# Flamingo gated block on one core: ScalarE's squares before its bank copies, output tiles one unit later, x1's statistics over four steps, another tail and beginning

## The chip, the cores and the metric

The kernel runs on one core of one Trainium2 chip. The metric is the device time of one execution in microseconds. The times before are from three executions; the trace is that of a fourth, profiled one.

## The reference

For eight batches b and an input x of 512 channels by 2048 positions:

```python
x = x + tanh(g_xattn) * xattn(layernorm(x), ctx, mask)     # gives x1
x = x + tanh(g_ffn) * ffn(layernorm(x))                    # layernorms run along the 2048 positions

def xattn(qk, v, mask):       # in windows of 128 positions, 8 heads of 32
    q, k, val = Wq @ qk + bq, Wk @ qk + bk, Wv @ v + bv    # 256 x 512 weights
    attn = softmax(q^T k / sqrt(32), masked)
    return (Wo @ gelu(attn applied to val) + bo) * mask

def ffn(x):                   # each of the 512 rows is 4 streams of 512
    logits = rms_norm(x) @ [W_res, W_pre, W_post]^T + base # 16 + 4 + 4 numbers a row
    H_res = (1-g) * I + g * sinkhorn(H_res_logits / 0.1, 50 iterations)   # 4 x 4 a row
    H_pre, H_post = softmax(...), softmax(...)
    y = (sum_n H_pre[n] * x[n]) @ W_branch                 # 512 x 512
    return H_res @ x_streams + H_post (outer) y
```

The output of a row tile is thus, for each of its four streams i: sum over j of cmat[i,j] * x1[j] + ccon[i] + post[i] * y, with the residual and the gates folded into the coefficients.

## The kernel before

The work is cut into 32 chunks G (eight batches, four chunks of 512 positions; `NG`, `CH`) and each chunk into eight units (four windows, two halves of the heads; `UPC = 8`). One loop over g, the unit, runs on every engine (`for g in range(FIRST, LAST)`), from 16 units ahead of the first attention unit to the end of the tail; NU = 256 is the number of attention units. What an engine does in unit g, and in which order, is written out by hand in the body of its loop; an engine executes its instructions in that order, and semaphores tie the engines together. r is the unit's number in its chunk, u its number in its batch (0 to 31).

In unit g TensorE makes the transposed scores of g-1 (`scores_t`), the values of g-2 (`values`, L816, L820), one or two products into a ring of four PSUM banks (`banked_at`: q of the next chunk at r = 0, 1, k at 2, 3, v at 4, 7, the output product at 5, 6, transposes of x1 at 3, 4, logits at 5), the scores of g+1, and parts of the branch product (`branch`, L831). ScalarE splits ctx and x into bf16 halves (`hi_ctx` L886, `norm_x` L892, `hi_x` L899), makes the exponential (`exp_scores` L931) and the inverse of the denominator (`inverse_den`, L938 and L940, `rden`), then the small tiles' work, the answers to VectorE's Sinkhorn (`answer`), the copies of the banks (`read_qk` L913, `read_v` L921, `copy_t` L963, `copy_pre` L1031, `copy_lg`), and last the squares of x1 (`square_x1`, L971; three of its four at r = 4) and `inverse_roots`. At r = 2 it also does gelu between two table loads. VectorE does the maximum (L1154), up to four Sinkhorn half-iterations (`half_at`, L1276 and L1277, between the others), the low part of q or k (`low_qk`, L1139) or the output's bias (`read_wo`, L1172), output tile parts (`output_parts`), `divide` (L1162) and statistics of x (L1125). GpSimd makes the low parts (L491, L496, L502), Newton steps and moments of the statistics (L516 to L562), the product kp of each Sinkhorn half for batches before the last (L575), `coefficients` (L587 to L596) and the DMA that adds x to x1 (L510). SP issues the DMAs in the order of its own loop, among them `load_x1t`, `store` and the q and k stacks.

The tiles of the second half: for each batch f four row tiles t. `TILE_AT` says in which unit a tile is at home, `BESIDE` (batches 0 to 5, beside the attention) and `BEHIND` (6 and 7, in the tail) say at which distance from it each part lies: `load` of x1, `first`, `xpre` and `pre` (the weighted sum of the streams and its transposes), `branch_0`, `branch_1`, `out_0`, `out_1` (ScalarE's first term of rows 0, 1 and of rows 2, 3, L1042), `stream_j` and `pair_j` (VectorE's further terms of rows 0, 1 and of rows 2, 3, L1305), `y` (L1321), `store`. In `BEHIND`, `diag` and `mix` make the transposed weighted sum directly on TensorE from diagonal matrices (L773, L775). With TILE_AT = 54 + 8t behind the batch's start, y stands at r = 0, xpre at r = 1, the streams of rows 0 and 1 at r = 6, 7 and 2, those of rows 2 and 3 at r = 3, 4, 5.

x1's statistics of a batch: `moments`, `inverse_roots`, `scale_b`, `inverse_roots`, `norm_b`, from unit STAT_AT = 12 on; the logits follow in unit 18 (`SOFTMAX_AT`), Sinkhorn from unit 23 to 48. In the last batch VectorE makes kp itself (L1266).

## Time and profile before

| | us |
|---|---|
| median of three executions | 1790.07 |
| lowest and highest | 1785.03, 1795.5 |
| profiled execution, its time | 1789.35 |
| profiled execution, span of the trace | 1787.5 |
| TensorE busy in the span | 1411.3 |
| VectorE busy | 1303.3 |
| ScalarE busy | 1133.5 |
| GpSimd busy | 808.1 |

Times in the rows are microseconds from the start of the span. The mean granted clock of TensorE was 0.91 of full speed. A timeline row tells start, duration, engine, line, operation, what is written and read, and in brackets how long the engine stood idle before it and who ended that.

### The profile page before, as it was taken

The page shows a single profiled execution, that of the slowest core. Times are in us where ns is not written, and L with a number is a line of the kernel's source. Part 1 is how long each engine was busy: PE and PEld are TensorE (multiplying, and loading weights), DVE is VectorE, ACT ScalarE, POOL GpSimd, SP SyncE. Part 2 cuts the span into 40 slices and gives each one's busy share as a digit, 9 for nine tenths or more (in the row PEclk, how much of TensorE's full clock was granted, in tenths as well). Part 3 has the DMA queues.
Part 4 walks back from the last instruction along what each step waited for, and adds up shares of the span by engine and source line. Part 5 has one row for each costly group of instructions (what it writes and reads, how often), then busy time and mean ns, then how long its engine had stood idle before and what let it go on. Part 6 is the DMA issues. An engine that isn't in the chain of part 4 may idle for free.

```text
span 1787.5 us, 36543 instructions
## 1 busy us (share of the span) xinstructions
PE 1411.3 (79%) x12736; PEld 882.2 (49%) x12736; DVE 1303.3 (73%) x3542; ACT 1133.5 (63%) x2305; POOL 808.1 (45%) x1373
## 2 busy tenths in 40 slices
PE   2679999988898888888888889888888897435335
PEld 0455566555555555554555455555555564224224
DVE  3244343566778888888788888887788878768988
ACT  2457878777677776777667767777777765322212
POOL 3323335355645564556555564556465634440000
PEclk9689999999999999999999999999999998657768
DMA  8456776666667766676676767676666554412123
GB/s 254 133 150 183 200 191 192 164 192 171 185 179 197 194 189 188 185 202 182 182 203 184 199 170 203 178 202 173 176 181 182 154 132 105 127 63 82 71 71 141
DMA packets 175462, 299.93 MB, mean 168 GB/s; under 512 B 25104, under 2 KB 76176, under 8 KB 171184
## 3 DMA queue, kind: packets, MB, share of 16 engines
q1 hardware_dynamic: 157872, 264.04, 48.9%
q0 software_dynamic: 17408, 33.56, 10.8%
q8 instruction: 102, 1.67, 0.4%
q14 instruction: 80, 0.66, 0.1%
HBM read 179.81 MB, written 67.11 MB: 138 GB/s over the span
## 4 chain that ended last, share of the span: by engine, by line
DVE 30%; PE 26%; ACT 14%; POOL 13%; issue 12%; SPq 3%; DMA 2%; DVEq 0%; POOLq 0%; ACTq 0%
PE pr L685 9%; PE pr L699 7%; POOL kp L575 7%; DVE ssum L1276 5%; ACT squares L971 3%; DVE sv L1277 3%; DVE otile_even L1305 3%; DVE xpre L1293 2%; POOL x1c L510 2%; DVE sa L1277 2%; DVE otile_odd L1305 2%; DVE otile_even L1321 2%; DVE x1c L1172 2%; PE av_ps L816 2%; DVE negm L1154 2%
## 5 line engine op out<-in xcount | busy, mean ns | idle before, releaser
L575 POOL TENSOR_TENSOR kp<-ke,sv 128x64 f32<-128x64 f32 x329 | 149.1, 453 | 282.9 <-DVE sv L1277 282.2
L1276 DVE TENSOR_REDUCE ssum<-kp 128x16 f32<-128x64 f32 x768 | 182.5, 238 | 123.5 <-POOL kp L575 116.7
L491 POOL TENSOR_TENSOR x_hl<-xc,x_hl 128x512 bf16<-128x512 f32 x128 | 156.3, 1221 | 153.3 <-ACT x_hl L899 153.3
L699 PE MATMUL pr<-wv,ctx_hl 128*128 128x256 bf16 x1536 | 195.7, 289 | 26.2 <-DVE k_hl L1139 20.2
L1162 DVE TENSOR_TENSOR o_sb<-av_ps,rden 128x128 f32<-128x128 f32 x256 | 72.8, 284 | 192.3 <-ACT rden L940 188.7
L575 POOL TENSOR_TENSOR kp<-ke,sa 128x64 f32<-128x64 f32 x343 | 149.4, 435 | 139.8 <-DVE sa L1277 139.8
L685 PE MATMUL pr<-x_hl,wq 128*128 128x512 bf16 x768 | 182.8, 389 | 35.3 <-POOL x_hl L491 35.3
L816 PE MATMUL av_ps<-probs,v_t 128*32 128x128 f32 x2048 | 111.6, 289 | 122.1 <-DVE o_sb L1162 121.7
L685 PE MATMUL pr<-x_hl,wk 128*128 128x512 bf16 x768 | 206.0, 426 | 0.0
L1154 DVE TENSOR_REDUCE negm<-s_ps 128x4 bf16<-128x512 f32 x256 | 166.8, 651 | 48.9 <-PE s_ps L789 48.2
L931 ACT ACTIVATE probs<-st_ps,key_bias 128x512 f32<-128x512 f32 x256 | 173.4, 677 | 37.3 <-PE st_ps L803 37.0
L712 PE MATMUL pr<-o_sb,wo 128*128 128x512 bf16 x768 | 190.7, 385 | 6.5 <-DVE x1c L1172 6.4
L699 PEld LDWEIGHTS pr<-wv,ctx_hl 128*128 128x128 bf16 x1536 | 153.7, 103 | 65.4 <-DVE k_hl L1139 25.5
L496 POOL TENSOR_TENSOR ctx_hl<-ctx_raw,ctx_hl 128x512 bf16<-128x512 f32 x128 | 147.6, 1162 | 41.8 <-ACT ctx_hl L886 41.8
L801 PE MATMUL st_ps<-q_st,k_st 96*128 96x128 bf16 x1024 | 148.2, 222 | 19.0 <-ACT probs L931 19.0
L1305 DVE SCALAR_TENSOR_TENSOR otile_even<-x1t_even,cmat,otile_even 128x512 f32<-128x512 f32 x192 | 148.8, 786 | 6.9 <-ACT otile_even L1042 6.6
L803 PE MATMUL st_ps<-id_bf,negm 128*128 128x128 bf16 x1024 | 147.4, 221 | 0.0
L1305 DVE SCALAR_TENSOR_TENSOR otile_odd<-x1t_odd,cmat,otile_odd 128x512 f32<-128x512 f32 x192 | 139.7, 751 | 1.2 <-ACT otile_odd L1042 0.5
L685 PEld LDWEIGHTS pr<-x_hl,wq 128*128 128x128 bf16 x768 | 71.9, 100 | 126.1 <-POOL x_hl L491 35.3
L685 PEld LDWEIGHTS pr<-x_hl,wk 128*128 128x128 bf16 x768 | 77.1, 107 | 109.4 <-issue 48.9
L831 PE MATMUL f<-wb,xpt 128*128 128x512 f32 x256 | 124.5, 616 | 7.9 <-ACT xpt L1031 4.8
L801 PEld LDWEIGHTS st_ps<-q_st,k_st 96*128 96x128 bf16 x1024 | 100.4, 99 | 61.4 <-ACT probs L931 47.1
(157 smaller groups left out, 3055.5 us busy)
## 6 DMA issues: line engine op xcount, KB each, us to landing
xs<-in_dram SPq DMA_DIRECT2D x128, 256.0 KB, 5.8
xc<-in_dram SPq DMA_DIRECT2D x128, 256.0 KB, 4.3
ctx_raw<-in_dram SPq DMA_DIRECT2D x32, 1024.0 KB, 7.7
x1c<-in_dram POOLq DMA_DIRECT2D x64, 512.0 KB, 7.6
x_dram<-x1c SPq DMA_DIRECT2D x32, 1024.0 KB, 5.1
q_st<-q_hl SPq DMA_DIRECT2D x384, 64.0 KB
k_st<-k_hl SPq DMA_DIRECT2D x384, 64.0 KB
x1t_even<-x_dram SPq DMA_DIRECT2D x16, 1024.0 KB, 5.9
```

The costliest lines, as they stand in the source:

```text
L491: nc.gpsimd.tensor_tensor(x_hl[:, G % 2, 1, t, :], xc[:, t, :], x_hl[:, G % 2, 0, t, :], ALU.subtract).then_inc(x_split, 1)
L496: ins = nc.gpsimd.tensor_tensor(ctx_hl[:, 1, t, :], ctx_raw[:, t, :], ctx_hl[:, 0, t, :], ALU.subtract)
L575: nc.gpsimd.tensor_tensor(kp[:], ke[:], v, ALU.mult).then_inc(kp_made, 1)
L685: ins = nc.tensor.matmul(bank(what)[:], w[:, a, t, i * P:(i + 1) * P], x_hl[:, G % 2, m, t, :], start=(t == 0 and a + m == 0), stop=(t == ...
L699: ins = nc.tensor.matmul(bank(what)[:, j * E:(j + 1) * E], ctx_hl[:, a, t, win], wv[:, m, t, :], start=(t == 0 and a + m == 0), stop=(t == ...
L712: ins = nc.tensor.matmul(bank(what)[:], wo[:, a, et, t * P:(t + 1) * P], o_part(G, et, m), start=(et == 0 and a + m == 0), stop=(et == ET ...
L801: nc.tensor.matmul(part, k_st[0:ROWS, G % 2, et, h, win], q_st[0:ROWS, G % 2, et, h, win], start=True, stop=False)
L803: ins = nc.tensor.matmul(part, negm[:, k % 2, h:h + 1].broadcast_to([P, P]), id_bf[:], start=False, stop=True)
L931: nc.scalar.activation(probs[:, k % 2, :], st_ps[:], ACT.Exp, bias=key_bias[:, b, w:w + 1], scale=SCALE).then_inc(exp_done, 1)
L1154: nc.vector.tensor_reduce(negm[:, k % 2, :], s_ps[:].rearrange("p (h j) -> p h j", h=HPT), AX.X, ALU.max, negate=True).then_inc(max_done, 1)
L1276: cf.link(nc.vector.tensor_reduce(s_t, k, AX.X, ALU.add))
L1305: ins = nc.vector.scalar_tensor_tensor(out=otile[n % 2][:, i, :], in0=x1t[n % 2][:, j * C:(j + 1) * C], scalar=cmat[:, f % 2, t, i, j:j + ...
```

## The change

- `SQUARES_AT` goes from [3, 4, 4, 4] to [3, 4, 4, 5], and on ScalarE `square_x1` moves ahead of the bank copies; `inverse_roots` moves ahead of the answers.
- The tiles of batches 0 to 5 get a home one unit later (55 + 8t); load, first, xpre and pre keep their unit, all other parts move by one.
- The statistics: both halves of `moments` at the end of unit 13, `inverse_roots` in 14 and 17, `scale_b` in 15 and 16, `norm_b` in 17 (before: 13, 13 and 14, 14, 16).
- Batch 6's tiles use `AMID`: rows 2 and 3 are computed on TensorE as four products of diagonal matrices with x1 (`mix_row`), from matrices that ScalarE makes (`diagonals_row`) and into a bank that it reads (`read_row`); VectorE then only adds y to these rows.
- The column sums of the weights (`csum`) are made a unit earlier, and the load of ctx's chunk 1 is issued behind the k stack of chunk 0.

```diff
--- before.py
+++ after.py
@@ -58,7 +58,7 @@
 HI_CTX_AT, LOW_CTX_AT = [0, 0, 1, 1], [1, 2, 2, 3]
 
 T_AT, LOGITS_AT, SELECT_AT = [3, 3, 4, 4], 5, 9
-SQUARES_AT = [3, 4, 4, 4]
+SQUARES_AT = [3, 4, 4, 5]
 
 
 STAT_AT = UPC + SQUARES_AT[-1]
@@ -69,15 +69,19 @@
 COEF_AT = SINK_AT + len(SINK)
 RETURN_AT = SINK_AT + SINK.index((RETURN, None))
 
-BESIDE = dict(load=-8, first=-6, xpre=-5, pre=-3, branch_0=0, branch_1=1, out_0=-1, out_1=0,
+BESIDE = dict(load=-9, first=-7, xpre=-6, pre=-4, branch_0=0, branch_1=1, out_0=-1, out_1=0,
               stream_1=0, stream_2=1, y=2, stream_3=4, pair_1=5, pair_2=6, pair_3=7, store_0=5, store_1=8)
 BEHIND = dict(load=-5, diag=-3, mix=-2, branch_0=-1, branch_1=-1, out_0=-1, out_1=0,
               stream_1=0, stream_2=1, y=2, stream_3=3, pair_1=3, pair_2=4, pair_3=5, store_0=4, store_1=6)
+
+AMID = dict(load=-5, diag=-3, mix=-2, branch_0=-1, branch_1=-1, diag_2=-2, diag_3=-1, row_2=-1, row_3=0,
+            out_0=-1, read_2=0, read_3=1, stream_1=0, stream_2=1, stream_3=2, y=3, store_0=4, store_1=5)
 LAST_BESIDE = B - 3
-TILE_AT = {(f, t): UNITS * (f + 1) + 54 + UPC * t for f in range(LAST_BESIDE + 1) for t in range(DT)}
+TILE_PARTS = [BESIDE] * (B - 2) + [AMID, BEHIND]
+TILE_AT = {(f, t): UNITS * (f + 1) + 55 + UPC * t for f in range(LAST_BESIDE + 1) for t in range(DT)}
 TILE_AT.update({(B - 2, t): NU + SINK_AT - 1 + 6 * t for t in range(DT)})
 TILE_AT.update({(B - 1, t): NU + SINK_AT + len(SINK) + 1 + 6 * t for t in range(DT)})
-assert COEF_AT < 54
+assert COEF_AT < 55
 LAST = TILE_AT[B - 1, DT - 1] + UPC
 XS = DT * 4
 XSN = 4
@@ -103,7 +107,7 @@
 
 
     return [(f, t) for (f, t), at in TILE_AT.items()
-            if g == at + (BESIDE if f <= LAST_BESIDE else BEHIND).get(part, LAST)]
+            if g == at + TILE_PARTS[f].get(part, LAST)]
 
 
 def sink_at(g):
@@ -142,7 +146,7 @@
     made += [("t", H, j) for H, j in at_step(g, 2, T_AT)]
     made += [("lg", H, 0) for H, j in at_step(g, 2, [LOGITS_AT])]
     made += [("pre", f, t) for f, t in tiles_at(g, "pre")]
-    if g == -1:
+    if g == -2:
         made.append(("csum", 0, 0))
     return made
 
@@ -193,6 +197,8 @@
 
         diag = ctx_raw[:, 0:2 * (N + 1) * P // CH + 1, :].rearrange("p t c -> p (t c)")[:, 0:2 * (N + 1) * P]
         diag = diag.rearrange("p (k n c) -> p k n c", k=2, n=N + 1)
+
+        diag_r = xc[:, 0:2 * N * P // CH, :].rearrange("p t c -> p (t c)").rearrange("p (k n c) -> p k n c", k=2, n=N)
         ctx_hl = sb("ctx_hl", [P, 2, DT, CH], BF16)
         x_hl = sb("x_hl", [P, 2, 2, DT, CH], BF16)
         q_hl = sb("q_hl", [P, 2, ET, CH], BF16)
@@ -341,6 +347,8 @@
         small_req = sem("small_req")
         small_done = sem("small_done")
         diag_made = sem("diag_made")
+        diag_r_made = sem("diag_r_made")
+        row_full = sem("row_full")
         xp_first = sem("xp_first")
         xpre_ready = sem("xpre_ready")
         y_full = sem("y_full")
@@ -469,7 +477,7 @@
                         sp.wait_ge(negrow_ready, 1)
                     sp.dma_start(k_st[ROWS:ROWS + 1, (G + 1) % 2].rearrange("p t h j -> p (t h) j"),
                                  bcast(neg_rows[G + 1:G + 2, :], 1, HEADS)).then_inc(stack_loaded[(G + 1) % 2], 16)
-                if r == 4 and 1 <= G + 2 < NG:
+                if r == (4 if G >= 0 else 5) and 1 <= G + 2 < NG:
                     sp.wait_ge(ctx_split, G + 2)
                     load_ctx(G + 2)
                 if r == 7 and NC <= G + 4 and G + 3 < NG:
@@ -621,10 +629,8 @@
                     add_x(G - 2, 1)
                 if g >= 0 and u == 15 and b + 1 < B:
                     xstat(b + 1)
-                for ready in ffn_at(g, STAT_AT + 1):
-                    moments(ready, 0)
-                for ready in ffn_at(g, STAT_AT + 2):
-                    scale_b(ready, 0)
+                for ready in ffn_at(g, STAT_AT + 3):
+                    scale_b(ready, 1)
                 scale_at(f, its, 2)
                 for H, t in low[1:]:
                     split_ctx(H, t)
@@ -635,10 +641,11 @@
                 if r not in (6, 7):
                     for H, t in at_step(g, -2, LOW_X_AT):
                         split_x(H, t)
-                for ready in ffn_at(g, STAT_AT + 1):
+                for ready in ffn_at(g, STAT_AT):
+                    moments(ready, 0)
                     moments(ready, 1)
                 for ready in ffn_at(g, STAT_AT + 2):
-                    scale_b(ready, 1)
+                    scale_b(ready, 0)
                 for ready in ffn_at(g, STAT_AT + 4):
                     norm_b(ready)
                 scale_at(f, its, 3)
@@ -775,6 +782,22 @@
                     ins = nc.tensor.matmul(block, ones[:], diag[:, n % 2, N, :], start=False, stop=True)
                 if part:
                     ins.then_inc(bank_full, 1)
+
+            def mix_row(f, t, i):
+
+                n, m = DT * f + t, 2 * t + i - 2
+                row = (s_ps, st_ps)[i % 2]
+                if m == 0:
+                    pe.wait_ge(max_done, NU)
+                    pe.wait_ge(exp_done, NU)
+                if m >= 2:
+                    pe.wait_ge(acc_ready, N * (n - 1) + i + 1)
+                pe.wait_ge(x1t_loaded[n % 2], 16 * (n // 2 + 1))
+                pe.wait_ge(diag_r_made, m + 1)
+                for j in range(N):
+                    ins = nc.tensor.matmul(row[:], diag_r[:, i % 2, j, :], x1t[n % 2][:, j * C:(j + 1) * C],
+                                           start=(j == 0), stop=(j == N - 1))
+                ins.then_inc(row_full, 1)
 
             def scores(k):
                 G, w, et = place(k)
@@ -868,6 +891,9 @@
                 for part in range(2):
                     for f, t in tiles_at(g, f"branch_{part}"):
                         branch(f, t, part)
+                for i in (2, 3):
+                    for f, t in tiles_at(g, f"row_{i}"):
+                        mix_row(f, t, i)
                 for what in banked_at(g + 1):
                     if what[0] == "sel":
                         bank_free(what)
@@ -1022,6 +1048,23 @@
                     nc.scalar.activation(diag[:, n % 2, i, :], id_sb[:], ACT.Identity, scale=pre[:, f % 3, t, i:i + 1])
                 nc.scalar.activation(diag[:, n % 2, N, :], id_sb[:], ACT.Identity, scale=rb[:, f % 3, 6, t:t + 1]
                                      ).then_inc(diag_made, 1)
+
+            def diagonals_row(f, t, i):
+                m = 2 * t + i - 2
+                if m == 0:
+                    act.wait_ge(coef_ready, 2 * f + 2)
+                    act.wait_ge(x_split, DT * NG)
+                if m >= 2:
+                    act.wait_ge(row_full, m - 1)
+                for j in range(N):
+                    ins = nc.scalar.activation(diag_r[:, i % 2, j, :], id_sb[:], ACT.Identity,
+                                               scale=cmat[:, f % 2, t, i, j:j + 1])
+                ins.then_inc(diag_r_made, 1)
+
+            def read_row(f, t, i):
+                act.wait_ge(row_full, 2 * t + i - 1)
+                nc.scalar.activation(otile[(DT * f + t) % 2][:, i, :], (s_ps, st_ps)[i % 2][:], ACT.Identity,
+                                     bias=ccon[:, f % 2, t, i:i + 1]).then_inc(acc_ready, 1)
 
             def copy_pre(what):
                 kind, f, t = what
@@ -1077,15 +1120,26 @@
                     first_products(done, t)
                 for done, t in tiles_at(g, "diag"):
                     diagonals(done, t)
+                for i in (2, 3):
+                    for done, t in tiles_at(g, f"diag_{i}"):
+                        diagonals_row(done, t, i)
                 for pair in range(2):
                     for done, t in tiles_at(g, f"out_{pair}"):
                         first_out(done, t, pair)
+                for i in (2, 3):
+                    for done, t in tiles_at(g, f"read_{i}"):
+                        read_row(done, t, i)
+                for n, at in enumerate((STAT_AT + 1, STAT_AT + 4)):
+                    for ready in ffn_at(g, at):
+                        inverse_roots(ready, n)
                 for n in range(5):
                     for ready in ffn_at(g, SOFTMAX_AT + n):
                         answer(ready, n)
                 for n in range(2):
                     for ready in ffn_at(g, RETURN_AT + n):
                         answer(ready, 5 + n)
+                for H, t in at_step(g, 2, SQUARES_AT):
+                    square_x1(H, t)
                 made = banked_at(g)
                 for n, what in enumerate(made):
                     if what[0] in "qk":
@@ -1098,8 +1152,6 @@
                         copy_lg(what)
                     elif what[0] in ("pre", "mix"):
                         copy_pre(what)
-                for H, t in at_step(g, 2, SQUARES_AT):
-                    square_x1(H, t)
                 if g == FIRST + UPC + 3:
                     w_parts(2, wv, wv_loaded)
                 if g == -2:
@@ -1108,9 +1160,6 @@
                     gelu(G - 1)
                 if g >= 0 and u == 14 and b + 1 < B:
                     xstat(b + 1)
-                for n in range(2):
-                    for ready in ffn_at(g, STAT_AT + 1 + n):
-                        inverse_roots(ready, n)
 
         @block.vector
         def _(dve):
@@ -1306,13 +1355,14 @@
                                                      scalar=cmat[:, f % 2, t, i, j:j + 1], in1=otile[n % 2][:, i, :],
                                                      op0=ALU.mult, op1=ALU.add)
                 if i % 2:
-                    if j == N - 1:
+                    if j == N - 1 and f != B - 2:
                         ins.then_inc(out_ready, 1)
                     else:
                         cf.link(ins)
 
             def add_y(f, t, half):
                 n = DT * f + t
+                last = f == B - 2
                 if half == 0:
                     dve.wait_ge(y_full, n + 1)
                 else:
@@ -1324,6 +1374,11 @@
                 if half:
                     ins.then_inc(y_read, 1)
                     dve.wait_ge(y_read, n + 1)
+                elif last:
+                    cf.link(ins)
+                if last:
+
+                    nc.vector.memset(spare[:, 1:2], 0.0).then_inc(out_ready, 1)
 
             def output_parts(g, half):
                 for j in range(1, N):
```

## Rows read from the trace of the kernel before

**Rows 1.** The page, first part: busy us, share of the span, instructions of each engine.
```profile
PE 1411.3 (79%) x12736; PEld 882.2 (49%) x12736; DVE 1303.3 (73%) x3542; ACT 1133.5 (63%) x2305; POOL 808.1 (45%) x1373
```
**Rows 2.** Table by stretch; columns: us, busy us (instructions) of each engine, clock, DMA.
```profile
229.00:266.00 37.00, 35.11 (x372) 22.21 (x370) 14.89 (x32) 30.08 (x61) 13.74 (x13) 1.00 0.72 195
711.00:760.00 49.00, 43.02 (x387) 25.68 (x386) 41.31 (x115) 34.89 (x68) 28.15 (x44) 0.93 0.67 186
...
1270.00:1450.00 180.00, 160.08 (x1548) 99.92 (x1547) 146.74 (x404) 134.54 (x276) 103.05 (x173) 0.99 0.64 172
```
**Rows 3.** Timeline of TensorE, 711 to 752 us: start, duration, instruction, idle before it.
```profile
722.07 0.43 PE L816 MATMUL av_ps<-probs,v_t 128*32 128x128 f32 x8 [1.90 <-DVE o_sb L1162]
...
737.04 4.46 PE L699 MATMUL pr<-wv,ctx_hl 128*128 128x256 bf16 x24 [1.85 <-DVE k_hl L1139]
```
**Rows 4.** Timeline of VectorE, steps 0 and 1 of the same chunk.
```profile
710.75 0.63 DVE L1154 TENSOR_REDUCE negm<-s_ps 128x4 bf16<-128x512 f32 x1
...
714.35 1.32 DVE L1321 SCALAR_TENSOR_TENSOR otile_even<-f,post,otile_even 128x512 f32<-128x512 f32 x2
...
716.37 0.63 DVE L1154 TENSOR_REDUCE negm<-s_ps 128x4 bf16<-128x512 f32 x1
...
720.61 1.11 DVE L1293 SCALAR_TENSOR_TENSOR xpre<-x1t_odd,pre,xpre 128x512 f32<-128x512 f32 x1
721.64 0.28 DVE L1162 TENSOR_TENSOR o_sb<-av_ps,rden 128x128 f32<-128x128 f32 x1
```
**Rows 5.** Timeline of ScalarE, step 4 of that chunk and the start of step 5.
```profile
741.54 0.60 ACT L921 ACTIVATE v_t<-pr 128x512 f32<-128x512 f32 x1 [3.71 <-PE pr L699]
...
743.18 0.72 ACT L971 ACTIVATE squares<-x1c,nmean 128x512 bf16<-128x512 f32 x1
...
745.29 0.81 ACT L892 ACTIVATE xc<-xc,ra 128x512 f32<-128x512 f32 x1
```
**Rows 6.** Timeline of VectorE, step 5 of that chunk.
```profile
747.88 0.29 DVE L1162 TENSOR_TENSOR o_sb<-av_ps,rden 128x128 f32<-128x128 f32 x1 [2.18 <-ACT rden L940]
```
**Rows 7.** Timeline of GpSimd, unit 13 of a batch: first and last of nine of moments.
```profile
646.57 0.48 POOL L541 TENSOR_TENSOR sums<-sums 128x8 f32<-128x8 f32 x2 [2.22 <-ACT squares L971]
...
649.59 0.23 POOL L550 TENSOR_SCALAR rb<-rb 128x4 f32<-128x4 f32 x1
```
**Rows 8.** Timeline of VectorE, unit 18 of a batch: softmax_first.
```profile
676.18 3.97 DVE L1219 SCALAR_TENSOR_TENSOR logit<-logit,rb,base_sb 128x32 f32<-128x32 f32 x4
```
**Rows 9.** Timeline of TensorE, a batch's first chunk: k's two products.
```profile
772.10 2.76 PE L685 MATMUL pr<-x_hl,wk 128*128 128x512 bf16 x12
...
778.07 4.45 PE L685 MATMUL pr<-x_hl,wk 128*128 128x512 bf16 x12
```
**Rows 10.** Timeline of TensorE and ScalarE in the tail, batch 6's first tile.
```profile
1613.16 3.70 PE L831 MATMUL f<-wb,xpt 128*128 128x512 f32 x8 [0.69 <-ACT xpt L1031]
...
1615.93 0.24 ACT L995 ACTIVATE ke<-zl 128x64 f32<-128x64 f32 x1
```
**Rows 11.** Timeline of VectorE in the tail: ends of three Sinkhorn half-iterations.
```profile
1632.48 0.25 DVE L1277 RECIPROCAL sa<-ssum 128x16 f32<-128x16 f32 x1
...
1633.33 0.25 DVE L1277 RECIPROCAL sv<-ssum 128x16 f32<-128x16 f32 x1
...
1634.58 0.25 DVE L1277 RECIPROCAL sa<-ssum 128x16 f32<-128x16 f32 x1
```
**Rows 12.** Timelines of SP, ScalarE and TensorE at the beginning.
```profile
61.26 0.43 SPq L388 DMA_DIRECT2D ctx_raw<-in_dram  x1
...
69.97 0.79 SPq L470 DMA_DIRECT2D k_st<-neg_rows  x1
...
67.84 1.15 ACT L886 ACTIVATE ctx_hl<-ctx_raw 128x512 bf16<-128x512 f32 x2 [4.10 <-DMA ctx_raw<-in_dram]
...
88.29 0.67 ACT L931 ACTIVATE probs<-st_ps,key_bias 128x512 f32<-128x512 f32 x1
...
73.16 6.98 PE L720 MATMUL pr<-wf,ones 128*128 128x32 f32 x32
```

## The prediction, made before the changed kernel was timed

> **What bounds the kernel now.** I read the page first: TensorE is 79% busy, VectorE 73%, ScalarE 63%, so no engine alone sets the span [rows 1]. The table by stretch shows what the second half of the computation costs: in a chunk of attention alone TensorE is busy for 35.1 of 37.0 us, a chunk that also carries an output tile and a Sinkhorn part takes 49 us with TensorE busy for 43.0 and VectorE for 41.3 [rows 2]. The idle time of TensorE inside such a chunk then tells which wait ends last: before `values` it waits 1.90 us for VectorE's `divide` (L1162), and before v's first product 1.85 us for `low_qk` (L1139) [rows 3]. After such waits the clock is granted at its lower level, 1.2 GHz of 2.4: the same twelve products take 4.45 us and not 2.76 [rows 9], and v's take 4.46 [rows 3]. So a chunk is a ring: VectorE's steps 6, 7, 0, 1 (a step is one unit of the loop; r is its number in the chunk of eight), then k's product and ScalarE's gelu with its two table loads in steps 2 and 3, then v's product in step 4, then ScalarE's squares, whose delay ends at VectorE's `divide` of step 5, idle for 2.18 us [rows 6]. Behind the chunks comes a tail, in which VectorE's Sinkhorn chain of the last batch and its multiplies follow each other nearly without a gap [rows 11].
>
> **Squares ahead of the copies (step 4).** ScalarE waits 3.71 us for v's product, copies v and two transposed tiles, and only then does three squares: 743.18 until the next norm at 745.29, 2.1 us; its `rden` then releases VectorE [rows 5, 6]. Two squares move into the 3.71 us wait, the third goes to step 5 behind `rden`. VectorE's maximum of step 6 comes 2.0 us earlier. TensorE itself gains nothing there, since its long waits are others [rows 3]; what counts is VectorE's start.
>
> **Tiles one unit later.** All out, branch, stream, y and store parts move; xpre, pre, first and load stay at the same step (their leads and the tile time shift by one each). Y goes from step 0 to step 1, where xpre already is. VectorE's step 0 takes 5.62 us from maximum to maximum, y's four multiplies being 2 x 1.32 us; step 1 takes 5.27 us to its `divide` [rows 4]. The row at 714.35 is the second pair. Step 0 then has stream_2's two multiplies for y's four, but its third half-iteration is set by GpSimd anyway, so I take 0.4 to 1.3 us off, value 0.5 (nearest: the y behind that half-iteration is cut from 1.32 to 0.66). Step 1 gains 4 x 0.66 = 2.64 us; between 2.2 (the third xpre multiply takes 1.11 us now, near 0.66 if it slips behind GpSimd's work) and 2.64, value 2.3. Net +1.8 on VectorE, which is nearly full in steps 6 to 1. Behind the waiting `divide` stand `values`, k's product and the gelu chain. Against the 2.0 us of the squares: 2.0 - 1.8 = 0.2 us gained a chunk, 21 chunks: **-4 us** (bounds -0.8 to +0.6 each: -17 to +13). TensorE's branch part (half of 3.70 us [rows 10]) moves from step 6 to 7 and from 7 to 0, and fills waits: nothing. The DMAs: the stores go one step later on SP's queue, and `load_x1t` now stands behind pair_3 of the same step; it lands about a step ahead of its reader, and what stands behind it on SP (an x chunk, x pieces) is read four steps later: nothing, at worst 1 us a chunk.
>
> Two engines and one port: a multiply with its operand in PSUM takes 0.66 us (two in 1.32), the third xpre multiply, with both in SBUF and GpSimd at work, 1.11 [rows 4]. The Trainium skill, SBUF — State Buffer, section "Who interferes with whom", says that a VectorE instruction with two SBUF inputs and a GpSimd instruction that reads SBUF exclude each other for their whole length, whereas one with a single SBUF input (y reads PSUM) does not. By it y in step 1 would be the cheap neighbour and the collision 2.2 us, without it 2.64; over 21 chunks 9 us.
>
> **First chunk of each batch.** There the low clock falls today on k's second product (778.07), while the first runs at 2.76, so the gelu chain starts early [rows 9]. With `divide` of step 1 later against TensorE (its branch part sits in step 0, so its wait grows from 1.90 towards 3 us), the slow product is the first, gelu starts 1.7 us later, and one square (0.7 us [rows 5]) now stands ahead of k's copy, for which low_qk and v's product wait. I take 0 to 3.2 us, value 1.6, in five batches: **+8 us**.
>
> **Statistics over four steps.** Today moments starts when the squares end: GpSimd runs 646.57 to 649.8, kp products among them, while ScalarE's `rden` is awaited anyway [rows 7]. Now moments waits for the fourth square in step 13, behind `rden`, and its 3.2 us stand ahead of the fourth half-iteration: in this chunk the 2.0 us of the squares are lost and about 1.0 more. Newton's four operations then share step 15 with xstat's seven (+0.6 by the same spacing), and steps 16 and 17 shift the rest; norm_b comes behind `coefficients`, which moves the ctx differences back by its five operations; beside those softmax_first needs 3.97 us for four tiny operations [rows 8], and they come later with it. Against the normal chunk +2.7 us (1 to 5), five times: **+13.5 us**.
>
> **Chunks without tiles.** TensorE is busy for 35.1 of 37.0 us in them [rows 2], so squares ahead of copies can give tenths, a little more in the three with Sinkhorn: **-2 us** (-4 to 0).
>
> **Beginning.** csum takes 6.98 us behind the first scores, ahead of q's product; a unit earlier it lies in the wait for the k stack. But the load of ctx(1), issued at 61.26, now stands behind that stack, whose last issue ends at 70.8; ScalarE's first split of ctx (67.84 now, 6.6 us behind the issue) moves to 78, and the first exp (88.29) comes behind it and two norms: 84.8 [rows 12]. **-3.5 us** (-7 to 0).
>
> **Tail.** For batch 6's four tiles rows 2 and 3 go to TensorE. VectorE loses six multiplies a tile. A half-iteration alone takes 0.85 us, one with a multiply 1.25 [rows 11]; I take 0.5 for a single one: four of them singly (4 x 0.5) and two behind others (1.2) make 3.2, less 0.3 for two small memsets and waits: -2.9 a tile, -11.6. TensorE gets eight fp32 matmuls of the branch's shape a tile (3.70 us for four calls, 7.4 for eight [rows 10]) in a stretch where it idles; ScalarE gets eight copies of the identity and two readings for two outputs. One of these readings is on the path: `read_row` (step 22 of the tail) stands ahead of answer 4 on ScalarE. Today the branch product starts at 1613.16 and answer 4 at 1615.93. Then the row follows the branch: 1613.2 + 3.7 + 3.7 + 0.6 = 1621.2, +5.3 us [rows 10]; at the low clock +12. Softmax_first +0.3. Sum **-6 us** (-12 to +4).
>
> Sum: -4 + 8 + 13.5 - 2 - 3.5 - 6 = +6. The profiled execution takes 1789.35 us for a span of 1787.5 (1.9 us around it), 0.7 us below the median of 1790.07. 1789.35 + 6 = 1795.4, with the 0.7 for the median: **1796 us**.
>
> **Rivals.** (a) The collision is absorbed: VectorE reaches step 1 early by the 2.0 us and GpSimd's waits swallow two of y's multiplies (0.5 us a chunk), and moments hides in the quiet of step 13 as today. Then a chunk gives 0.2 + 0.5 us, 15 in 21, and statistics and batch heads cost 6 us and not 21.5: 1790.05 - 15 + 6 - 11.5 = 1770. For it: VectorE is busy for only 41.3 of 49 us, its waits for GpSimd's kp among the rest [rows 2]; against it: the rows of step 1 leave hardly a gap [rows 4]. (b) Slower: TensorE's longer wait at step 2 brings the low clock into chunks that escape it now. It decides where a wait reaches the length of those behind which the clock is low today, 1.90 and 1.85 us, and each case costs 4.45 - 2.76 = 1.7 us [rows 3, 9]. Today the mean granted clock is 0.93 in such a chunk and 0.99 from 1270 to 1450 us, when the x statistics have ended [rows 2]: there it can get worse. Some 12 more of them: 1796 + 20 = 1816. For it: the wait grows; against: a chunk that has it already pays nothing new. (c) It doesn't do what it says: the squares' time isn't regained as `rden` is followed at once by another wait, chunks neutral apart from moments, the row tiles win nothing as the answers wait again at iteration 25: about 1800.
>
> **How the numbers follow.** Forecast 0.40, spread 1785 to 1806; (a) 0.25, 1762 to 1782; (b) 0.25, 1798 to 1828; (c) 0.10, 1790 to 1808. About 0.5% is what a measurement of this kernel tells from no change: below 1781.1, between, above 1799.0. From the first case 0.02 / 0.24 / 0.14, (a) 0.23 / 0.02 / 0, (b) 0 / 0.03 / 0.22, (c) 0.01 / 0.05 / 0.04: faster 0.26, same 0.34, slower 0.40. The range of 1768 to 1820 leaves out about 0.1 on either side; the forecast's own is 1785 to 1806.
>
> **What would show it.** Right: squares ahead of v's copy in step 4, `divide` of step 5 with no idle time before it; wait before `values` of step 2 of 2.5 to 3.5 us; step 1 of VectorE near 9 us; in the chunk of moments a fourth half-iteration that waits 3 us for GpSimd; in the tail answer 4 some 5 us further behind the branch product, and then a Sinkhorn stretch 11 to 12 us shorter. Wrong: if chunks take 47 to 48 us (a), or if the mean granted clock falls below 0.93, and from 1270 us on above all (b). An x1t tile that lands behind `first_products` would refute my nothing for the DMAs.

## The result, and the profile of the changed kernel

The changed kernel takes **1820.9 us** (1818.4 to 1825.0) against 1791.6 for the kernel before in the same comparison: **1.016 times its time, interval 1.013 to 1.019**. The forecast was 1796 us within 1768 to 1820, so the time lies just outside, on the slow side. Its profiled execution has a span of 1816.0 us, mean granted clock 0.908.

First the page, which answers to [rows 1], and the table by stretch, which answers to [rows 2] (same columns). The first line of the table is the chunk of [rows 2], a batch's fourth, and the second the stretch from 1270 us, as there. The third line is the first chunk of a batch, the last two are the chunks with x1's statistics:

```profile
PE 1439.9 (79%) x12644; PEld 902.0 (50%) x12800; DVE 1275.0 (70%) x3526; ACT 1144.2 (63%) x2337; POOL 780.4 (43%) x1373
```
```profile
710.00:758.00 48.00, 41.55 (x384) 25.73 (x386) 40.57 (x115) 34.80 (x69) 26.29 (x44) 0.93 0.67 185
1270.00:1450.00 180.00, 154.66 (x1387) 94.03 (x1406) 137.50 (x374) 128.22 (x260) 90.50 (x153) 0.92 0.56 160
758.00:805.00 47.00, 40.20 (x380) 24.48 (x388) 38.56 (x108) 34.81 (x71) 22.97 (x37) 0.96 0.70 198
805.00:860.00 55.00, 44.19 (x394) 26.26 (x401) 41.22 (x120) 36.75 (x76) 30.70 (x65) 0.91 0.63 185
860.00:911.00 51.00, 44.76 (x383) 28.41 (x386) 38.59 (x94) 33.38 (x72) 22.67 (x37) 0.90 0.59 170
```

The ordinary chunk is a little shorter (48 us, was 49). The two chunks of the statistics take 55 and 51 us, and the stretch from 1270 us has a clock of 0.92 where it had 0.99. TensorE is busy for 28.6 us more by the page, but 25 of them lie in the tail, where it now makes rows, so the page alone doesn't show what the chunks lost.

The starts of `negm` in VectorE's timeline, eight to a chunk, cut the span so (chunks counted from 0; c mod 4 = 0 is a batch's first). The last column gives the forecast for the same stretch, from its terms. "Tail" is all that follows the last maximum.

| stretch | before | after | change | forecast |
|---|---|---|---|---|
| to the first maximum | 80.3 | 71.8 | -8.5 | -3.5 |
| chunks 0 to 6 | 267.8 | 266.1 | -1.7 | -2 with the next line |
| chunks 7 to 11 | 217.6 | 218.9 | +1.3 | |
| chunk c mod 4 = 0, mean of 12 to 24 | 46.3 | 47.4 | +1.1 | +1.4 |
| c mod 4 = 1 and 2 together, means | 99.0 | 105.8 | +6.9 | +2.3 |
| c mod 4 = 3, mean | 49.4 | 47.95 | -1.45 | -0.2 |
| chunks 12 to 25, sum | 681.6 | 706.1 | +24.5 | +14 |
| chunks 26 to 30 | 228.2 | 244.2 | +16.0 | +3 |
| last eight steps | 35.3 | 36.6 | +1.3 | |
| tail | 276.7 | 272.4 | -4.3 | -6 |

Now the lines themselves. VectorE in the chunk from 709.6 us, step 1 (compare [rows 4]) and step 5 (compare [rows 6]):

```profile
716.92 1.32 DVE L1371 SCALAR_TENSOR_TENSOR otile_even<-f,post,otile_even 128x512 f32<-128x512 f32 x2
718.15 1.68 DVE L1342 SCALAR_TENSOR_TENSOR xpre<-x1t_odd,pre,xpre 128x512 f32<-128x512 f32 x2
...
720.28 1.32 DVE L1371 SCALAR_TENSOR_TENSOR otile_even<-f,post,otile_even 128x512 f32<-128x512 f32 x2
721.64 0.75 DVE L1342 SCALAR_TENSOR_TENSOR xpre<-x1t_odd,pre,xpre 128x512 f32<-128x512 f32 x1
722.31 0.28 DVE L1211 TENSOR_TENSOR o_sb<-av_ps,rden 128x128 f32<-128x128 f32 x1
...
745.90 0.29 DVE L1211 TENSOR_TENSOR o_sb<-av_ps,rden 128x128 f32<-128x128 f32 x1 [0.27 <-ACT rden L966]
```

Y's four multiplies stand among xpre's three, and `divide` behind them. In step 5 `divide` waits 0.27 us, where it waited 2.18. ScalarE shows why (compare [rows 5]): two squares now stand ahead of v's copy, in the time in which ScalarE waits for v's product.

```profile
736.72 0.71 ACT L997 ACTIVATE squares<-x1c,nmean 128x512 bf16<-128x512 f32 x1
...
737.42 0.70 ACT L997 ACTIVATE squares<-x1c,nmean 128x512 bf16<-128x512 f32 x1
...
741.29 0.60 ACT L947 ACTIVATE v_t<-pr 128x512 f32<-128x512 f32 x1 [3.07 <-PE pr L706]
```

TensorE in that chunk (compare [rows 3]) and in the next (compare [rows 9]):

```profile
722.74 0.43 PE L839 MATMUL av_ps<-probs,v_t 128*32 128x128 f32 x8 [2.80 <-DVE o_sb L1211]
...
735.96 5.30 PE L706 MATMUL pr<-wv,ctx_hl 128*128 128x256 bf16 x24 [1.85 <-DVE k_hl L1188]
...
771.33 0.43 PE L839 MATMUL av_ps<-probs,v_t 128*32 128x128 f32 x8 [3.59 <-DVE o_sb L1211]
771.91 4.45 PE L692 MATMUL pr<-x_hl,wk 128*128 128x512 bf16 x12
```

The wait before `values` of step 2 grew to 2.8 and 3.6 us. A product of v, 2.8 us at the full clock and 4.46 in [rows 3], now takes 5.3: all 24 of its matmuls run at 1.2 GHz (they start 0.21 us apart, and the granted clock is half from 735.0 to 741.8 us), 2.5 us dearer.

One sum is used from here on, the **low excess**. It is taken over the 57 products of k and v in steps 2 to 4 of chunks 12 to 30 (two of k and one of v a chunk), and adds up what each product takes above 2.8 us. It is 36.5 us before and **55.1 after**. Products over 3.3 us number 24 before (17 of k, 7 of v) and 29 after (14 of k, 15 of v, eight of these 5.3 us).

### The profile page after: what moved, and what is told of

It is laid out like the page before. It is cut to its first block, busy times and chain, and to the rows that moved or that the text cites. A ratio compares the mean times of both kernels' runs of the same rounds, so it can differ in the third digit from the quotient of the medians.

```text
span 1816.0 us, 36500 instructions
## 1 busy us (share of the span) xinstructions
PE 1439.9 (79%) x12644; PEld 902.0 (50%) x12800; DVE 1275.0 (70%) x3526; ACT 1144.2 (63%) x2337; POOL 780.4 (43%) x1373
## 3 DMA queue, kind: packets, MB, share of 16 engines
q1 hardware_dynamic: 157872, 264.04, 47.2%
## 4 chain that ended last, share of the span: by engine, by line
DVE 28%; PE 26%; POOL 15%; ACT 14%; issue 12%; SPq 3%; DMA 2%; DVEq 0%; POOLq 0%; ACTq 0%
PE pr L692 7%; POOL kp L583 7%; PE pr L706 7%; DVE ssum L1325 5%; POOL x1c L518 3%; PE pr L719 2%; DVE xpre L1342 2%; DVE sv L1326 2%; DVE otile_even L1371 2%; ACT g_sb L975 2%; DVE sa L1326 2%; ACT L970 2%; ACT probs L957 2%; DVE otile_even L1354 2%; ACT o_sb L982 2%
## 5 line engine op out<-in xcount | busy, mean ns | idle before, releaser
L583 POOL TENSOR_TENSOR kp<-ke,sv 128x64 f32<-128x64 f32 x329 | 136.4, 415 | 288.3 <-DVE sv L1326 288.3
L706 PE MATMUL pr<-wv,ctx_hl 128*128 128x256 bf16 x1536 | 219.9, 311 | 34.6 <-DVE k_hl L1188 29.6
L583 POOL TENSOR_TENSOR kp<-ke,sa 128x64 f32<-128x64 f32 x343 | 141.5, 413 | 195.4 <-DVE sa L1326 194.8
L499 POOL TENSOR_TENSOR x_hl<-xc,x_hl 128x512 bf16<-128x512 f32 x128 | 148.9, 1164 | 156.3 <-ACT x_hl L925 156.2
L692 PE MATMUL pr<-x_hl,wq 128*128 128x512 bf16 x707 | 175.0, 393 | 43.0 <-POOL x_hl L499 36.1
L706 PEld LDWEIGHTS pr<-wv,ctx_hl 128*128 128x128 bf16 x1536 | 165.2, 111 | 84.4 <-DVE k_hl L1188 35.4
L692 PE MATMUL pr<-x_hl,wk 128*128 128x512 bf16 x736 | 195.1, 421 | 5.0 <-issue 4.9
L1211 DVE TENSOR_TENSOR o_sb<-av_ps,rden 128x128 f32<-128x128 f32 x256 | 71.8, 280 | 179.4 <-ACT rden L966 176.4
L719 PE MATMUL pr<-o_sb,wo 128*128 128x512 bf16 x705 | 181.4, 385 | 11.4 <-issue 5.2
L1354 DVE SCALAR_TENSOR_TENSOR otile_even<-x1t_even,cmat,otile_even 128x512 f32<-128x512 f32 x180 | 131.4, 737 | 7.1 <-ACT otile_even L1085 6.8
L854 PE MATMUL f<-wb,xpt 128*128 128x512 f32 x256 | 124.5, 616 | 12.5 <-DVE otile_odd L1371 6.1
L1354 DVE SCALAR_TENSOR_TENSOR otile_odd<-x1t_odd,cmat,otile_odd 128x512 f32<-128x512 f32 x180 | 125.5, 719 | 1.4 <-ACT otile_odd L1085 0.6
```

The lines of the kernel that those rows point to most:

```text
L499: nc.gpsimd.tensor_tensor(x_hl[:, G % 2, 1, t, :], xc[:, t, :], x_hl[:, G % 2, 0, t, :], ALU.subtract).then_inc(x_split, 1)
L583: nc.gpsimd.tensor_tensor(kp[:], ke[:], v, ALU.mult).then_inc(kp_made, 1)
L692: ins = nc.tensor.matmul(bank(what)[:], w[:, a, t, i * P:(i + 1) * P], x_hl[:, G % 2, m, t, :], start=(t == 0 and a + m == 0), stop=(t == ...
L706: ins = nc.tensor.matmul(bank(what)[:, j * E:(j + 1) * E], ctx_hl[:, a, t, win], wv[:, m, t, :], start=(t == 0 and a + m == 0), stop=(t == ...
L719: ins = nc.tensor.matmul(bank(what)[:], wo[:, a, et, t * P:(t + 1) * P], o_part(G, et, m), start=(et == 0 and a + m == 0), stop=(et == ET ...
L1354: ins = nc.vector.scalar_tensor_tensor(out=otile[n % 2][:, i, :], in0=x1t[n % 2][:, j * C:(j + 1) * C], scalar=cmat[:, f % 2, t, i, j:j + ...
```

## Experiments

All times below are medians; the kernel before took 1788.9 us beside e1 to e4, 1795.6 beside e5 to e8, 1789.3 beside e9 to e12 and 1791.8 beside e13 to e15, so differences across these groups are uncertain by some us. The spans of the profiled executions bear the main ones out (after 1816.0, e4 1773.8, e5 1734.1, e7 1744.4, e9 1718.8, e12 1764.5, e13 1796.0). The low excess, in us, is the sum defined above; it is part of the time and overlaps with waits, so it is not a share that can be taken off exactly.

| kernel | us | ratio, interval | low excess |
|---|---|---|---|
| after | 1820.9 | 1.016 (1.013-1.019) | 55 |
| e1: after, tiles at the old unit | 1772.4 | 0.991 (0.988-0.993) | 20 |
| e2: after, square 3 behind the copy | 1812.7 | 1.013 (1.010-1.015) | 47 |
| e3: after, statistics as before | 1786.9 | 0.999 (0.998-1.000) | 39 |
| e4: ends alone | 1776.5 | 0.994 (0.992-0.995) | 35 |
| e5: e4 + squares ahead | 1734.5 | 0.965 (0.964-0.967) | 15 |
| e6: e5, square 3 behind | 1736.1 | 0.967 (0.964-0.969) | 15 |
| e7: after, xpre in step 2 | 1748.2 | 0.974 (0.972-0.976) | 15 |
| e8: e5, fourth square in step 5 | 1752.6 | 0.977 (0.974-0.980) | 14 |
| e9: e3, xpre in step 2 | **1725.5** | 0.965 (0.961-0.969) | 22 |
| e10: e5, xpre in step 2 | 1746.9 | 0.977 (0.973-0.981) | 27 |
| e11: e5 with the old tail | 1739.5 | 0.973 (0.969-0.978) | 18 |
| e12: e5 + 1.3 us in step 1 | 1766.5 | 0.988 (0.984-0.992) | 39 |
| e13: e5 + 2.65 us in step 1 | 1796.3 | 1.003 (1.001-1.005) | 47 |
| e14: before + 1.3 us in step 1 | 1812.5 | 1.013 (1.009-1.017) | 29 |
| e15: e3, y in step 2 | 1729.5 | 0.967 (0.964-0.970) | 15 |

**One part undone at a time.** The tiles:

```diff
-BESIDE = dict(load=-9, first=-7, xpre=-6, pre=-4, ...
+BESIDE = dict(load=-8, first=-6, xpre=-5, pre=-3, ...
-TILE_AT = ... 55 + UPC * t
+TILE_AT = ... 54 + UPC * t
```

> The changed kernel with the output tiles back at their old unit (y in step 0, xpre in step 1 of a chunk), all else changed. Theory A (y beside xpre is the main cost): in the changed kernel step 1 of VectorE takes 9.0 us against 6.5, step 0 5.0 against 5.65, so 1.9 us a chunk in 20 chunks, 38 us, should come back: about 1782 us, and step 1 back at 6.5 us. Theory B (the new order on ScalarE puts TensorE's products of step 4 at the lower clock, whatever the tiles do): v's product of step 4 still takes 5.3 us in half of the chunks, only some 10 us come back: about 1810 us.

It came to 1772.4 us, 49 below the changed kernel: more than theory A's 38. Step 1 of an ordinary chunk is back at 6.52 us. The low excess falls by 35 us, so most of what comes back is time at the low clock, and theory B is out.

The square of step 3 goes behind k's copy:

```diff
-                for H, t in at_step(g, 2, SQUARES_AT):
+                for H, t in at_step(g, 2, SQUARES_AT) if r != 3 else []:
                     square_x1(H, t)
                 made = banked_at(g)
...
+                for H, t in at_step(g, 2, SQUARES_AT) if r == 3 else []:
+                    square_x1(H, t)
```

> The changed kernel with the square of step 3 behind k's copy, as in the kernel before; those of steps 4 and 5 stay ahead of the copies. Theory A (the square ahead of k's copy delays low_qk and v's product by 0.8 us, and this wait sends v's product to the lower clock, 5.3 us and not 2.8): in the chunks 0 and 2 of a batch the wait before v's product falls from 1.1 to 0.4 us and the product takes 2.8 us; with 0.8 us for the square and 2.5 us for the clock in about 8 chunks, 20 to 30 us come back: about 1797 us. Theory B (v's product is slow because of what TensorE did in the steps before, the later branch part among it): the wait shrinks by 0.8 us, the product stays at 5.3 us: 1812 us, or more where the square moves behind the first exp of the step.

1812.7 us, 8 less: theory B's figure. In the third chunk of a batch (c mod 4 = 2) v's product still takes 5.30 us in chunks 14, 18 and 22, behind waits of 0.91, 1.11 and 1.12 us. But of the 15 slow products of v three are gone, and of the eight at 5.3 us four, and the first chunk of a batch is 0.8 us shorter (47.4 to 46.6). So the square ahead of k's copy isn't the main cause of the slow products, and in this kernel it isn't free either.

The statistics: moments again in GpSimd's second and third part of unit 13, inverse roots at the end of ScalarE's units 13 and 14, both scales in unit 14.

```diff
-SQUARES_AT = [3, 4, 4, 5]
+SQUARES_AT = [3, 4, 4, 4]
...
-                for ready in ffn_at(g, STAT_AT):
-                    moments(ready, 0)
+                for ready in ffn_at(g, STAT_AT + 1):
                     moments(ready, 1)
```

> The changed kernel with x1's statistics and the third square of step 4 as in the kernel before (moments in the second and third half-iteration, the squares still ahead of the bank copies, three of them in v's wait). Theory A (moments behind the fourth square costs the chunk its 2 us and 0.7 more in step 5, 1 us in step 7 and 0.8 us in step 3): 4 us in each of 5 to 6 batches, about 1800 us, with step 5 of the chunk near 5.5 us. Theory B (moments lies beside a wait either way): within 3 us of 1821, and the third square makes the wait for rden of step 5 0.7 us longer in all other chunks: up to 1830 us.

1786.9 us, 34 below. Chunks 1 and 2 of a batch are back at 51.7 and 47.7 (sum 99.3; 105.8 in the changed kernel, 99.0 before). Theory A was right in kind and 40% short. The low excess falls by 16 us.

The ends alone are e1 and e3 together, with the squares behind the copies again (the diff of the whole change without its other parts):

> The kernel before with only the new beginning (csum a unit earlier, the load of ctx(1) behind the k stack) and the new tail of batch 6 (rows 2 and 3 of its tiles on TensorE). Theory A (the ends act alone): the first maximum 8.5 us earlier and the tail 4.3 us shorter as in the changed kernel, chunks between as before: 1791.6 - 12.8 = 1779 us. Theory B (part of the gain at the ends came from the squares or the later tiles, which leave ScalarE free at the tail's start): beginning -8.5 us, tail within 1 us of before: 1783 us.

1776.5 us, 12.4 below the kernel before: theory A. The first maximum comes at 71.7 us, chunks 12 to 30 take 909.4 us against 909.8, the tail 269.0 against 276.7. Chunk 0 takes 43.2 us there and 38.3 in the changed kernel with the same work (38.8 before), so the beginning's net gain lies between 4 and 9 us; why chunk 0 differs wasn't followed.

**The parts put on one by one.** Squares alone, on e4:

```diff
+                for H, t in at_step(g, 2, SQUARES_AT):
+                    square_x1(H, t)
                 made = banked_at(g)
...
-                for H, t in at_step(g, 2, SQUARES_AT):
-                    square_x1(H, t)
```

> The kernel before with the new ends and the squares ahead of the bank copies, three of them in the wait for v's product (step 4); tiles and x1's statistics as in the kernel before. Theory A (the three parts of the change act mostly by themselves: the squares gain, tiles and statistics cost): the two kernels with the squares ahead and one of the other parts undone lie 48 and 34 us below the changed kernel, whose chunks then leave 186 us a batch against 194.6: 1776.5 - 8 us in 4 to 5 batches = 1740 us, step 5 near 5.4 us. Theory B (the gain of the squares is used up at the next wait, on GpSimd or on TensorE at its lower clock, once the third square is in step 4): within 8 us of 1776.

1734.5 us, **42 us below e4**: theory A. A batch of four chunks takes 185.3 us against 194.6; step 5 falls from 7.4 to 5.5. The low excess falls from 35 to 15, half of the 42 us. TensorE in the second chunk of a batch shows how. The kernel before, from 811 us:

```profile
811.92 0.43 PE L816 MATMUL av_ps<-probs,v_t 128*32 128x128 f32 x8 [1.24 <-DVE o_sb L1162]
...
817.84 0.43 PE L816 MATMUL av_ps<-probs,v_t 128*32 128x128 f32 x8 [1.89 <-DVE o_sb L1162]
818.42 4.45 PE L685 MATMUL pr<-x_hl,wk 128*128 128x512 bf16 x12
```

and e5, from 786 us, where the wait of 1.24 us a step earlier is gone (VectorE's step 5, a few steps ahead, is 2 us shorter):

```profile
794.98 0.43 PE L840 MATMUL av_ps<-probs,v_t 128*32 128x128 f32 x8 [1.85 <-DVE o_sb L1212]
795.56 2.76 PE L693 MATMUL pr<-x_hl,wk 128*128 128x512 bf16 x12
...
809.05 2.79 PE L707 MATMUL pr<-wv,ctx_hl 128*128 128x256 bf16 x24 [1.85 <-DVE k_hl L1189]
```

The same wait of 1.9 us stands before a product at the low clock in one kernel and at the full clock in the other. The second of them is v's, 4.40 us in that chunk of the kernel before.

The same edit as in e2, now on e5:

> As e5_squares_ahead_alone, with the square of step 3 behind k's copy. Theory A (the square ahead of k's copy delays v's product): 0.8 us in each of 22 chunks, up to 17 us faster than e5. Theory B (the square finds its place in ScalarE's idle time only ahead of the copy, and behind it stands in front of the next exp): 0 to 8 us slower than e5. With the changed kernel the same edit brought 8 us.

1736.1 us, the interval overlaps e5's: theory B. On the old tiles the place of this square is worth nothing measurable, unlike in the changed kernel (e2).

The fourth square moved, the rest of the statistics left:

```diff
-SQUARES_AT = [3, 4, 4, 4]
-STAT_AT = UPC + SQUARES_AT[-1]
+SQUARES_AT = [3, 4, 4, 5]
+STAT_AT = UPC + 4
```

> As e5_squares_ahead_alone, with the third square of step 4 moved to step 5 as in the changed kernel, but moments, inverse roots and scales in the units of the kernel before. Theory A (moments' place ahead of the fourth half-iteration is what the statistics cost, not the square in step 5): within 4 us of e5. Theory B (any moments behind the fourth square costs, since it comes behind rden in step 5 and GpSimd's queue waits for it): 3 to 4 us in each of 7 batches, 20 to 25 us slower than e5.

1752.6 us, 18 more than e5: theory B in mechanism, 2 us under its figure. Nearly all of it lies in the chunk of moments: step 5 takes 8.82 us in it against 5.91, in six batches. GpSimd waits for the square, and VectorE for GpSimd (e8, their timelines at 816 to 822 us):

```profile
820.40 0.48 POOL L549 TENSOR_TENSOR sums<-sums 128x8 f32<-128x8 f32 x2 [3.36 <-ACT squares L998]
```
```profile
822.18 0.22 DVE L1326 TENSOR_REDUCE ssum<-kp 128x16 f32<-128x64 f32 x1 [3.99 <-POOL kp L583]
```

Between e8 and e1 lies the rest, moments in the fourth half-iteration and the scales' new units: another 20 us, of which 2.45 us a batch fall in the chunk behind (46.6 to 49.1) and 1.3 in the one after it (45.8 to 47.2). The changed kernel in the first two, on GpSimd and VectorE (compare [rows 7] for moments):

```profile
843.46 0.48 POOL L549 TENSOR_TENSOR sums<-sums 128x8 f32<-128x8 f32 x2 [1.96 <-ACT squares L997]
...
845.78 0.23 POOL L558 TENSOR_SCALAR rb<-rb 128x4 f32<-128x4 f32 x1
...
862.72 0.64 POOL L567 TENSOR_TENSOR rb<-rb 128x4 f32<-128x4 f32 x1
...
864.21 0.29 POOL L583 TENSOR_TENSOR kp<-ke,sv 128x64 f32<-128x64 f32 x1
```
```profile
846.30 0.27 DVE L1325 TENSOR_REDUCE ssum<-kp 128x16 f32<-128x64 f32 x1 [2.63 <-POOL kp L583]
...
864.53 0.22 DVE L1325 TENSOR_REDUCE ssum<-kp 128x16 f32<-128x64 f32 x1 [1.66 <-POOL kp L583]
```

Moments costs VectorE a wait of 2.63 us at once, and `scale_b` of half 1, now in unit 16 ahead of a `kp`, another 1.66. The first wait isn't new. In the kernel before it stood one half-iteration earlier in the same step:

```profile
842.97 0.22 DVE L1276 TENSOR_REDUCE ssum<-kp 128x16 f32<-128x64 f32 x1 [2.83 <-POOL kp L575]
```

There step 5 was long in all chunks, 7.4 us on average, and 7.7 in the one with moments. In the changed kernel it falls to 5.5 or less in the others, and stays at 8.1 in the one with moments, which misses the gain of the squares. With moments as before it falls too, to 5.9 (e5).

**What the collision in step 1 is.** Xpre's multiplies move out of it, into step 2:

```diff
-BESIDE = dict(load=-9, first=-7, xpre=-6, pre=-4, ...
+BESIDE = dict(load=-9, first=-7, xpre=-5, pre=-4, ...
```

> The changed kernel with xpre's multiplies a unit later, in step 2, while y stays in step 1. Theory A (both in one step is the cost; TensorE waits for the divide behind them before k's product): step 1 falls from 9.0 to 6.7 us, step 2 grows by 1 us at most, since VectorE idled there: 1.3 us in 20 chunks or more, below 1795 us. Theory B (VectorE's work of steps 6 to 2 is the ring, wherever it stands): step 2 grows by the same 2.3 us, and the k projections behind it are 2 us later: 1815 to 1825 us.

1748.2 us, **73 below the changed kernel** by one number: theory A in kind, which had asked for some 26 us. In a batch's fourth chunk steps 1 and 2 take 6.60 and 6.00 us instead of 8.98 and 4.66, 1.0 us less. Over chunks 12 to 30, which are 68 us shorter, these two steps give only 14 us. Steps 3 and 4, which follow k's and v's products, give 48 (7.2 and 6.5 us on average before the edit, 5.85 and 5.4 with it). The low excess falls by 40 us. With the statistics undone too (e9), and with y moved in place of xpre (e15: `xpre=-6`, `y=3`):

> The changed kernel with the statistics as before and xpre's multiplies in step 2 (both undoings together). Theory A (the statistics' place costs by itself, whether or not the tiles collide): they cost 18 to 20 us beside e5 and the kernel with the old tiles, so 1748 - 19 = 1729 us. Theory B (the statistics were dear only where TensorE was already at the lower clock, 34 us beside the colliding tiles): within 5 us of 1748.

> The changed kernel with the statistics as before and y's multiplies in step 2, xpre's staying in step 1. Theory A (only the length of step 1 counts, not which of the two leaves it): within 8 us of e9_tiles_late_xpre_2, 1717 to 1733 us. Theory B (y in step 2 stands behind TensorE's q and k work and holds the x1 tile and the products' bank longer, or 2.7 us are too much for step 2): 1740 us or more.

1725.5 and 1729.5 us: theory A in both (e9 some 4 us under its figure). The statistics cost 23 us here (e7 against e9), 34 beside the collision and 38 on the old tiles (e1 against e5). e9 is the fastest kernel of the study by its median, 3.5% under the kernel before; the ratios of e5 and e9 can't be told apart. Which of the two leaves step 1 matters little. On the old tiles, where step 1 isn't overfull, the same move (`xpre=-5` to `xpre=-4`) loses:

> As e5_squares_ahead_alone (tiles at the old unit, y in step 0), with xpre's multiplies in step 2. Theory A (what stands between the maximum of step 6 and the divide before k's product decides, so less in step 1 is a gain): step 1 falls from 6.5 to 4.3 us, TensorE's wait before `values` of step 2 vanishes, step 2 grows from 5.5 to 7: chunks 1 us shorter, 1734 - 20 = 1714 us. Theory B (the work only moves; steps 1 and 2 keep their sum of 12 us, k's second product and gelu come no earlier): 1730 to 1738 us.

1746.9 us, 12 more than e5 and outside both theories. The two steps together take 12.4 us against 12.0 in an ordinary chunk and 15.1 against 13.7 in a batch's third, and more products of k are at the low clock (18 for 9; low excess 27). Why wasn't followed further.

Last, a dose: work of known length on VectorE ahead of `divide`, its result unused. A reduction takes 0.67 us, and stands in step 1 of 22 chunks; e13 has four for the two shown.

```diff
+                if r == 1 and 80 < g < NU:
+                    for n in range(2):
+                        nc.vector.tensor_reduce(dose[...], id_sb ..., AX.X, ALU.max)
```

> As e5_squares_ahead_alone, with two idle reductions of 0.65 us each on VectorE in step 1 of 22 chunks, behind xpre and ahead of the divide; their result is not used. They are a dose of 1.3 us where y's multiplies came to stand. Theory A (the dose stretches TensorE's wait before `values` from 1.9 to 3.2 us, and k's product behind it goes to the lower clock, 4.45 us and not 2.76, in most chunks): 1.3 + 1.7 us and more in 20 chunks, 1790 us or above. Theory B (the dose costs itself at most; k's product stays at 2.8 us): up to 22 x 1.3 = 29 us, at most 1763 us. In theory A the collision needs no contention of y with xpre to explain the loss.

> As e12_dose_in_step_1 with four of the idle reductions, 2.65 us, in step 1: as much as y's four multiplies. Theory A (the later tiles cost 52 us, 1735 to 1787 us, through VectorE's time in step 1 alone): near the kernel with later tiles and the statistics as before, 1787 us; since no multiply leaves step 0 here, up to 0.6 us a chunk more, 1787 to 1800 us. Theory B (the later tiles cost also by TensorE's branch products in steps 7 and 0, or by y and xpre slowing each other): the dose stays clearly below, 1775 us or less.

> The kernel before with the 1.3 us dose of e12 in step 1. Its first k product of most chunks is at the lower clock already. Theory A (what was lost to the clock isn't lost twice): the dose costs itself and no more, 1.3 us in 16 chunks with xpre in step 1 or in all 22, 21 to 29 us: 1811 to 1819 us. Theory B (further products go to the lower clock, as from 1270 us on): 1.46 us a chunk as in e12 or more, 1821 us and above.

e12 came to 1766.5 us, 32 more than e5: between its theories, A in mechanism and less in size. By the profiles chunks 12 to 30 alone are 31 us longer. The second chunk of a batch in e12, against e5's above:

```profile
806.00 0.43 PE L841 MATMUL av_ps<-probs,v_t 128*32 128x128 f32 x8 [3.07 <-DVE o_sb L1213]
806.58 4.45 PE L694 MATMUL pr<-x_hl,wk 128*128 128x512 bf16 x12
...
820.98 4.15 PE L708 MATMUL pr<-wv,ctx_hl 128*128 128x256 bf16 x24 [1.85 <-DVE k_hl L1190]
```

The wait grows from 1.85 to 3.07 us, and both products fall to the low clock. Over the kernel the low excess grows by 23 us of the 32. e13, as long as y's multiplies, came to 1796.3: theory A, 9 us above the later tiles of e3, which take work out of step 0 in exchange. So the 52 us between e5 and e3 need neither TensorE's moved branch products nor any slowing of y and xpre by each other; that these do nothing isn't shown. e14, the same 1.3 us in the kernel before, costs 20.6 us, a third less than in e5: theory A. There the product was slow already, and the low excess doesn't grow (29 us, 36 before).

**The tail.** Squares ahead and the new beginning in the kernel before, nothing else:

> As e5_squares_ahead_alone, with batch 6's tiles at the tail as in the kernel before (all rows on VectorE). Theory A (the new tail is a gain in itself of 4 to 8 us, as the tails of 272.4 and 269.0 us against 276.7 say): 1734 + 6 = 1740 us. Theory B (TensorE's rows give nothing, the tails differ by the clock alone): within 2 us of 1734.

1739.5 us, 5 more than e5, ratio 0.973 for 0.965: theory A. The tails are 276.8 and 272.1 us.

## Why the prediction was wrong

**The step that failed: TensorE's clock was put at nothing in the sum.** The sum took microseconds of VectorE and GpSimd as microseconds of the kernel, part by part, and had the clock only in a rival. By place it missed in two stretches, both from the first table: the third chunk of a batch (c mod 4 = 2), +3.1 us (47.6 to 50.7) for -0.2, as the statistics' 2.7 us were set on the second, and chunks 26 to 30, +16.0 for +3. Just there the low excess grew, from 3.2 to 12.5 us in chunks 14, 18 and 22 and from 4.1 to 14.5 in chunks 26 to 30; elsewhere it grew and fell by about the same. In the three third chunks this needs two parts at once: with the tiles back (e1) it is 0.0 there, with the statistics back (e3) 2.5. **The second step that failed is the term of the statistics**, 13.5 us for what measured 23 to 38; it follows below.

**Squares: right.** ScalarE's order, the 2.0 us and the vanished wait of step 5 are as told. Alone they bring 42 us, which is 21 times 2.0. But that the size fits is luck: half of it is low excess that went away, while the forecast said "TensorE itself gains nothing there, since its long waits are others". The rows of e5 show one of those other waits gone and the product behind it at the full clock.

**Tiles later: right on VectorE, wrong at the next engine.** Step 1 grew by 2.5 us (forecast 2.3), step 0 shrank by 0.6 (0.5). The sum of 1.8 us, 38 in 21 chunks, was set against the squares' 2.0, and 8 us were added for the first chunks of the batches. In fact what is taken off again also takes back the full clock: the move costs 49 us (e1) or 52 (e3 against e5), 2.4 a chunk in 22, of which 24 us are low excess.

**Rival (b) was nearer.** It named the mechanism, had a chance of 0.25, and the 1820.9 us lie in its 1798 to 1828. Its sign came too: the clock from 1270 us on fell from 0.99 to 0.92. In detail it was off. It had some 12 more slow products at 1.7 us each, the price of k's. There are five more in all, fewer of k (14 for 17), and v's is what fell from 1270 us on, in all five chunks there and in none before, 1.5 to 2.5 us dearer. Of the 41 us that the chunks and last steps lost together, 18.6 are low excess.

By the rule weighed in the forecast (the Trainium skill, SBUF — State Buffer, "Who interferes with whom") the collision would be 2.2 us, without it 2.64. Step 1 grew by 2.5, the dose of 2.65 us, which reads one input, by 2.4: the runs don't tell the two apart. What the trace shows beside it agrees with the rule: y's first pair, with one input in PSUM, took 1.32 us, as before, while GpSimd worked on x's low part (1.16 us from 717.34).

**First chunk of a batch: right**, +1.1 us for +1.4. The slow product is the first of k now (771.91), as told. Of the square ahead of k's copy e6 says that it is free on the old tiles, and e2 that it is worth 0.8 us in this chunk of the changed kernel.

**Chunks without tiles: -0.4 us for -2** (chunks 0 to 11). Chunk 9 already has moments beside Sinkhorn and takes 43.4 us, 41.3 before and 40.7 in e5.

**Statistics: mis-sized by more than half and miscounted; the largest miss in the sum.** The forecast had 2.7 us in five batches, 13.5. Six batches carry them beside Sinkhorn (chunks 9, 13, ... 29). The fourth square costs 2.9 us in step 5 (e8; 3.0 forecast). Missing was the chunk behind, 2.5 us, for which some tenths were taken. The rows show 1.66 us of it, `scale_b` ahead of a `kp`; that the rest is `norm_b` behind `coefficients` isn't shown. Altogether they cost 38 us on the old tiles (e1 against e5, low excess +4), 34 in the changed kernel (low excess +16) and 23 with xpre in step 2 (e7 against e9). So most of this miss is the term itself and not the clock.

**Beginning: right in mechanism, too careful in size.** The first maximum comes 8.5 us earlier, outside the bounds of -7 to 0; net of chunk 0 it is 4 to 9 us (e4). The load of ctx(1) was issued at 69.88 us and its split began at 74.94, 5.1 us later; the forecast took 78. The first exp stands 5.4 us behind that split, where 6.8 were taken (compare [rows 12]):

```profile
74.94 1.15 ACT L912 ACTIVATE ctx_hl<-ctx_raw 128x512 bf16<-128x512 f32 x2 [7.02 <-DMA ctx_raw<-in_dram]
...
80.34 0.67 ACT L957 ACTIVATE probs<-st_ps,key_bias 128x512 f32<-128x512 f32 x1
```

That is 8.0 us earlier than before.

**Tail: right within its bounds**, -4.3 for -6. Answer 4 stands behind the row (compare [rows 10]): branch at 1649.40, answer at 1657.15, 7.75 us apart against 2.77, +5.0 for +5.3.

```profile
1656.57 0.69 ACT L1066 ACTIVATE otile_even<-s_ps,ccon 128x512 f32<-128x512 f32 x1 [4.55 <-PE s_ps L798]
1657.15 0.25 ACT L1021 ACTIVATE ke<-zl 128x64 f32<-128x64 f32 x1
```

From the first half-iteration behind it (1657.43; 1616.63 before) to the end of the span it takes 158.6 us against 170.9: -12.3 for -11.6. What keeps the tail at -4.3 is 3.4 us more ahead of the branch product, which weren't followed; with old statistics, tiles and squares (e4) the tail is 7.7 us shorter.

**DMAs: nothing in the chunks; one tile lands late.** The x1t tile is issued at 751.94 us in the chunk above (745.88 before), and no instruction in the chunks waits for such a load. But the sign that the forecast named did come for one tile, batch 5's last, at the start of the tail:

```profile
1586.68 0.81 ACT L1037 ACTIVATE xpre<-x1t_odd,rb,pre 128x512 f32<-128x512 f32 x1 [7.01 <-DMA x1t_odd<-x_dram]
```

The wait was 4.07 us before. It is 6.8 to 8.0 us in all kernels with the later tiles and 2.7 to 4.1 in the others. The tails don't follow it (268.5 us with 6.8 in e9, 272.1 with 3.8 in e5), so no cost of it is shown.

The sum of +6 thus was +29: the ends -12.8 for -9.5, all between them +41.4 for +15.5. By undoing, the parts between come to +44: -42 and +52 for the squares and tiles, where +4 was said with the first chunks, and +34 for the statistics, where +13.5 was said. The low excess and the statistics' second chunk and sixth batch overlap in this, so no exact split is claimed.

## What to carry to other kernels

Where products behind waits run at the lower clock, a microsecond on the path is not worth a microsecond: 1.3 us of dose cost 1.46 us a chunk in a kernel mostly at the full clock (low excess 15) and 0.94 in one that was low more often (36), and the parts of a change don't add. So before summing, list for each product which clock it has and what wait stands before it, and price the part in the state that the other parts leave. A part that frees an engine and a part that fills the same stretch again should be tried apart: here the squares alone were worth 2.4%, and the whole change lost 1.6%.

## What the runs showed of the hardware

A wait's length alone doesn't say which clock follows it. Behind 1.9 us k's product took 4.45 us in the kernel before and 2.76 in e5, where the engine hadn't waited the 1.24 us one step earlier. Behind 3.07 us it took 4.45 (e12) and 3.75 (e14, chunk of the same place); in e14 the two groups of small products just ahead of it already took 0.66 and 0.69 us, 0.43 each at the full clock, so the lower clock had begun earlier. V's product behind 1.85 us took 2.79, 4.46 and 5.30 in different kernels. That what the engine did over the steps before counts along with the last wait is how these rows read; they don't give a rule for how much.
